# Two groups of value sums in a row, every eight steps, in a three-stage attention kernel

## The chip, the cores and the metric

The kernel runs on one core of one Trainium2 chip. The metric is the device time of one execution in microseconds; times of instructions come from one profiled execution.

## What is computed

Tokens (16 sequences of 512, width 128) are embedded, mixed by a low-rank attention, and sent through a block with three attentions of 8 heads of 16: a "spatial" one (S) and a causal "temporal" one (T), whose weights a router picks per sequence, and a cross attention (C) between their outputs. A feed-forward layer follows.

```python
att = jax.nn.softmax(jnp.einsum('bthd,bshd->bhts', q, k), axis=-1)
o = jnp.einsum('bhts,bshd->bthd', att, v).reshape(B, T, D)
...
spatial_out = _spatial_experts(xn, idx_s, ...)
temporal_out = _temporal_experts(xt, idx_t, ...)
fused = _cross_mha(spatial_out, temporal_out, ...)
x = x + fused
```

## The kernel before

Three programs run one after the other: `embed_and_mix`, `attend` and `feed_forward`. The change lies in `attend`, which takes most of the time. Its work is 48 units: S, T and C for each of 16 sequences, and a unit has 32 tiles (8 heads by 4 blocks of 128 tokens).

Each engine runs a list written out by hand. Time is counted in slots of 32 steps; three slots make a batch (`units` says which sequences meet in a slot). In a slot TensorE (PE) scores one unit (`score`, line 1265, bf16, one tile per step), makes the logits of the unit scored in the slot before (`logits`, line 1285, tile n - 8 at step n, so the last eight tiles fall into the first eight steps of the next slot), and weighs the values with its probabilities (`weigh`, line 1304). I call a slot by the unit that is scored in it: in the T slot T is scored, and the logits and sums are first C's and then S's; in the C slot they are S's, then T's; in the S slot T's, then C's. At a step the order on PE is: transpose of the maxima (1274), projections of the next unit (1248 and 1252, steps 3, 9 and 12 to 15), logits, group of sums, score, output projection (1321 and 1324, steps 29 and 30).

- **Scores** go to a ring of `RL` = 3 PSUM banks. VectorE (DVE) reduces each to its row maxima (`reduce`, lines 1066 and 1070); the score of tile n waits until tile n - 3 has been reduced.
- **Logits** go to a second ring of `RC` = 3 banks. ScalarE (ACT) turns them into probabilities in SBUF (`exponential`, line 1170); the logits of tile n wait for the exponential of tile n - 3. Causal T tiles are narrower (512, 384, 256 or 128 columns).
- **Groups.** Four tiles of probabilities make a group, 8 groups a unit. `weigh` runs four fp32 matmuls with 32 columns of weights each, side by side in the array, into one PSUM bank (`sums`). A T group also waits for GpSimd (POOL) to zero the future on its diagonal block (`zero_future`, line 939). The probabilities have `RP` = 3 buffers of one group each, so the first exponential of a group waits for the sums of the group three before it.
- **Evictions.** After groups 3 and 7 ACT empties the bank: a Ln (`s_all`, `s_high`) and, one exponential later, a copy (`u_all`, `u_high`). Groups 0 and 4 wait for these. DVE then shuffles the sums (`swap`, step 21), ACT takes the reciprocal (`reciprocal`, step 24), and POOL multiplies.

Two rules of waiting that the steps below rest on:

```python
at_least(pe, reduced, TILES * u + n - RL + 1)      # in score
at_least(pe, exped, TILES * u + n - RC + 1)        # in logits
pe.wait_ge(exped, TILES * u + 4 * q + 4)           # in weigh, S and C
pe.wait_ge(cut, 2 * NB * b + q + 1)                # in weigh, T
at_least(act, summed, 8 * u + n // 4 - RP + 1)     # in exponential, n % 4 == 0
```

In the order before, group q is weighed at step 17 + 4q: groups 0 to 3 at steps 17, 21, 25 and 29 of a slot, groups 4 to 7 at steps 1, 5, 9 and 13 of the next. The evictions stand at ACT's steps 30 and 31 (groups 0 to 3) and 14 and 15 (groups 4 to 7).

Of the kernel before, what the change touches and what calls it, by code (L numbers as in the profile page):

```python
# [38 lines left out]
TURN_AT, KEEP_MAXIMA_AT = (19, 6), (18, 5)  # L39
PROJECT_AT = (3, 9, 12)  # L40
KEPT_AT = (4, 10)
WEIGH_AFTER = 9
VALUES_AT = 16
GROUP_1_AT, GROUP_2_AT = (30, 31), (14, 15)
SWAP_AT, RECIP_AT = 21, 24
OUTPUT_AT, KEEP_AT = 29, 31
PROJECT_PARTS, OUTPUT_PARTS = (1, 1, 4), 2
LAG = 8
# [20 lines left out]
def exists(b):  # L69
    return not isinstance(b, int) or 0 <= b < B  # L70
# [14 lines left out]
def desk_use(name, b):  # L85

    if name[0] in "qkv" and name[1] == "S" and isinstance(b, int) and b == 0:
        return "qkv".index(name[0])
    i = b - DESK_BATCH[name]
    order = [u for s in DESK for u in s]  # L90
    at = order.index(name)
    if isinstance(i, int):
        return desk_count(i) + sum(exists(i + DESK_BATCH[u]) for u in order[:at])
    return DESK_FIRST + DESK_USES * (i - STEADY[0]) + at


def unit_no(kind, b):

    if kind == "C":
        return 3 * B - 1 if isinstance(b, int) and b == B - 1 else 3 * b + 4  # L100
    if isinstance(b, int) and b == 0:
        return "ST".index(kind)
    return 3 * b - 1 + "ST".index(kind)
# [10 lines left out]
def group_place(kind, b, q):  # L114

    return ring_place(kind, b, 4 * q, 4 * RP) // 4


def at_least(eng, sem, value):

    if not isinstance(value, int) or value > 0:
        eng.wait_ge(sem, value)
# [568 lines left out]
def attend(nc, shared, s_in, s_out, t_in, t_out, c_in, c_out, c_bias):  # L691
# [3 lines left out]
    with ExitStack() as ctx:  # L695
# [90 lines left out]
        def units(i, slot):  # L786

            return ((("T", i), ("S", i), ("C", i - 2), ("T", i - 1)),
                    (("C", i - 1), ("T", i), ("S", i), ("C", i - 2)),
                    (("S", i + 1), ("C", i - 1), ("T", i), ("S", i)))[slot]  # L790
# [19 lines left out]
        def first_key(kind, tile):  # L810

            return P * (tile // 4 % NB) if kind == "T" else 0
# [41 lines left out]
        with nc.Block() as block:  # L854
# [370 lines left out]
            def _(pe):  # L1225
# [31 lines left out]
                def score(kind, b, n):  # L1257

                    u = unit_no(kind, b)
                    if n == 0:  # L1260
                        pe.wait_ge(stack_in[kind], 16 * 2 * NPROD * (b + 1))
                    at_least(pe, reduced, TILES * u + n - RL + 1)
                    hd, tb = n // NB, n % NB
                    keys = P * (tb + 1) if kind == "T" else T
                    nc.tensor.matmul(psum[:, ring_place(kind, b, n, RL), 0:keys], qs[kind][0:RA, hd, P * tb:P * tb + P],  # L1265
                                     ks[kind][0:RA, hd, 0:keys], start=True, stop=True).then_inc(scored, 1)

                def turn_maxima(kind, b, half):

                    if not exists(b):  # L1270
                        return
                    pe.wait_ge(reduced, TILES * unit_no(kind, b) + HALF * (half + 1))
                    at_least(pe, desk_free, desk_use("hm"[half] + kind, b))
                    nc.tensor.transpose(desk[0:HALF, 0:P], mx[kind][:, HALF * half:HALF * half + HALF], ident[:])\
                        .then_inc(desk_full, 1)

                def logits(kind, b, n):

                    u = unit_no(kind, b)
                    if n % HALF == 0:  # L1280
                        pe.wait_ge(rows_in[n // HALF][kind], 16 * NPART * (b + 1))
                    at_least(pe, exped, TILES * u + n - RC + 1)
                    hd, s, t0 = n // 16 * 4 + n % 4, n // 4 % NB, first_key(kind, n)
                    bank = LOGITS + ring_place(kind, b, n, RC)
                    nc.tensor.matmul(psum[:, bank, t0:T], ks[kind][0:RB, hd, P * s:P * s + P],  # L1285
                                     qs[kind][0:RB, hd, t0:T], start=True, stop=True).then_inc(logits_in, 1)

                def weigh(kind, b, q):

                    u = unit_no(kind, b)  # L1290
                    g, s = q // NB, q % NB
                    if kind == "T":
                        pe.wait_ge(cut, 2 * NB * b + q + 1)
                    else:
                        pe.wait_ge(exped, TILES * u + 4 * q + 4)
                    if q == 0:
                        pe.wait_ge(v_ready[kind], b + 1)
                        pe.wait_ge(desk_free, desk_use("v" + kind, b) + 1)
                        at_least(pe, high_out, u)
                    if q == NB:  # L1300
                        pe.wait_ge(low_out, u + 1)
                    t0 = first_key(kind, 4 * q)
                    for j in range(4):
                        last = nc.tensor.matmul(sums[32 * j:32 * j + 32, t0:T], va[kind][:, s, g, j, :],  # L1304
                                                probs[:, group_place(kind, b, q), j, t0:T], start=(s == 0),
                                                stop=(kind == "T" or s == NB - 1), skip_group_check=(kind == "T"))
                    last.then_inc(summed, 1)
# [21 lines left out]
                def slot_program(i, slot):  # L1329
                    (kn, bn), (ka, ba), (kb, bb), (ko, bo) = units(i, slot)  # L1330
                    for n in range(TILES):
                        if n == TURN_AT[0]:
                            turn_maxima(ka, ba, 0)
                        if n == TURN_AT[1]:
                            turn_maxima(kb, bb, 1)
                        for c in range(3):
                            if 0 <= n - PROJECT_AT[c] < PROJECT_PARTS[c]:
                                project(kn, bn, c, n - PROJECT_AT[c])
                        if n < LAG and exists(bo):
                            logits(ko, bo, TILES - LAG + n)  # L1340
                        if n >= LAG and exists(bb):
                            logits(kb, bb, n - LAG)
                        q, rest = divmod(n - LAG - WEIGH_AFTER, 4)
                        if rest == 0 and q < 0 and exists(bo):
                            weigh(ko, bo, q + 8)
                        if rest == 0 and q >= 0 and exists(bb):
                            weigh(kb, bb, q)
                        if exists(ba):
                            score(ka, ba, n)
                        if 0 <= n - OUTPUT_AT < OUTPUT_PARTS and exists(bo) and ko != "S":  # L1350
                            output(ko, bo, n - OUTPUT_AT)
# [14 lines left out]
                last.then_inc(folded, 1)  # L1366
                pe.wait_ge(fold_kept, 2)
                whole_loop(pe, slot_program)


# [247 lines left out]
```

## Time and profile before

| | before |
|---|---|
| median of 3 runs (lowest to highest) | 1627.6 us (1627.55 to 1627.78) |
| the profiled execution's own time | 1629.0 us |
| its span, first to last instruction | 1627.2 us |
| PE busy | 1510.4 us (93%) |
| DVE busy | 1241.3 us (76%) |
| ACT busy | 1129.1 us (69%) |
| POOL busy | 1000.1 us (61%) |
| mean granted clock of PE | 0.947 |

The busy times are those of the whole span, with the first and the last program in them. A matmul's row lasts until its last result is written, and the next one starts before that; the time that a matmul holds the array is therefore read from one start to the next, not from the length of the row. Start to start is what the text uses.

### The profile page before, as it was taken

What the parts mean: (1) busy time and instruction counts of PE and PEld (TensorE: products, weight loads), DVE (VectorE), ACT (ScalarE), POOL (GpSimd) and SP (SyncE); (2) the same over time, 40 slices, a digit from 0 to 9 for tenths busy, and PEclk for the clock granted to TensorE, in tenths of its full rate; (3) what the DMA queues carried; (4) which work ended last, traced back from release to release, by engine and by line L of the source; (5) the groups of instructions that cost most, each with busy time, mean ns of one, the idle gap of its engine ahead of it and who ended that gap; (6) DMA issues with size and microseconds to landing.
All of it is one profiled execution on the core that took longest, in us unless ns stands there. A gap on an engine that the chain in (4) does not pass through costs nothing. (4 is left out here: it accounts for less than half of the span.)

```text
span 1627.2 us, 37445 instructions
## 1 busy us (share of the span) xinstructions
PE 1510.4 (93%) x8694; PEld 661.2 (41%) x8694; DVE 1241.3 (76%) x3412; ACT 1129.1 (69%) x2201; POOL 1000.1 (61%) x1359
## 2 busy tenths in 40 slices
PE   4779948899999999999999999999999999975999
PEld 1239932233333333343333333333333343211777
DVE  6868858579888887979888887979788888452772
ACT  5756734567787878787787878787787878824433
POOL 7704443856777776866767776856767775432553
PEclk9879958889999999999999999999999999967999
DMA  3311153645654655655655655655655643030222
GB/s 83 105 31 46 46 81 50 87 71 74 80 81 61 88 69 65 86 69 72 80 77 64 88 65 69 85 68 74 80 75 66 88 59 64 2 40 28 59 71 65
DMA packets 140021, 110.34 MB, mean 68 GB/s; under 512 B 22721, under 2 KB 134465, under 8 KB 139969
## 3 DMA queue, kind: packets, MB, share of 16 engines
q1 hardware_dynamic: 137920, 105.53, 44.0%
q0 software_dynamic: 2048, 4.20, 1.0%
q8 instruction: 23, 0.38, 0.1%
q14 instruction: 30, 0.24, 0.1%
HBM read 19.29 MB, written 8.39 MB: 17 GB/s over the span
## 5 line engine op out<-in xcount | busy, mean ns | idle before, releaser
L1170 ACT ACTIVATE probs<-psum 128x512 f32<-128x512 f32 (+3 forms) x1536 | 755.2, 548 | 226.8 <-PE psum L1285 216.2
L1070 DVE TENSOR_REDUCE mx_S<-psum 128x1 f32<-128x512 f32 x512 | 326.2, 681 | 47.5 <-PE psum L1265 45.8
L1070 DVE TENSOR_REDUCE mx_C<-psum 128x1 f32<-128x512 f32 x512 | 317.8, 676 | 45.1 <-PE psum L1265 45.1
L1066 DVE CUSTOM_DVE_ANT_0 psum<-psum,causal 128x128 f32<-128x128 f32 (+3 forms) x512 | 242.8, 510 | 100.6 <-PE psum L1265 97.8
L1265 PE MATMUL psum<-ks_S,qs_S 96*128 96x512 bf16 x512 | 196.9, 395 | 10.3 <-DMA ks_S<-parts_k 6.0
L1265 PE MATMUL psum<-ks_C,qs_C 96*128 96x512 bf16 x512 | 199.6, 398 | 4.3 <-DMA ks_C<-parts_k 1.2
L1285 PE MATMUL psum<-qs_C,ks_C 99*128 99x512 bf16 x512 | 189.3, 385 | 3.6 <-ACT probs L1170 3.2
L1285 PE MATMUL psum<-qs_S,ks_S 99*128 99x512 bf16 x512 | 190.6, 384 | 0.2
L951 POOL CAST parts_q<-f_q 128x512 bf16<-128x512 f32 x48 | 29.3, 610 | 227.6 <-ACT f_q L1161 227.1
L1265 PE MATMUL psum<-ks_T,qs_T 96*128 96x128 bf16 (+3 forms) x512 | 156.7, 309 | 1.7 <-DVE mx_S L1070 0.9
L1285 PE MATMUL psum<-qs_T,ks_T 99*128 99x256 bf16 (+3 forms) x512 | 153.3, 305 | 2.1 <-ACT probs L1170 1.0
L1304 PE MATMUL psum<-probs,va_S 128*32 128x512 f32 x1024 | 136.4, 604 | 1.7 <-ACT u_all L1190 0.6
L1304 PE MATMUL psum<-probs,va_C 128*32 128x512 f32 x1024 | 136.9, 607 | 0.8 <-ACT u_all L1190 0.6
L1265 PEld LDWEIGHTS psum<-ks_C,qs_C 96*128 96x128 bf16 x512 | 49.8, 97 | 166.6 <-DVE mx_C L1070 124.2
L939 POOL TENSOR_SCALAR_AFFINE_SELECT probs<-probs 128x512 f32<-128x512 f32 x128 | 81.0, 633 | 56.6 <-ACT probs L1170 54.5
L1265 PEld LDWEIGHTS psum<-ks_S,qs_S 96*128 96x128 bf16 x512 | 50.1, 98 | 153.5 <-DVE mx_S L1070 104.4
L1265 PEld LDWEIGHTS psum<-ks_T,qs_T 96*128 96x128 bf16 x512 | 50.5, 99 | 137.0 <-DVE mx_T L1066 93.0
L1304 PE MATMUL psum<-probs,va_T 128*32 128x512 f32 (+3 forms) x1024 | 97.7, 454 | 2.4 <-POOL probs L939 1.4
L1517 ACT ACTIVATE gT<-psum,b 128x512 f32<-128x512 f32 x64 | 44.0, 687 | 80.4 <-PE psum L1537 80.4
L1005 POOL TENSOR_TENSOR s_all<-s_all,s_high 128x512 f32<-128x512 f32 x48 | 60.9, 1269 | 23.4 <-ACT u_high L1180 23.4
L316 POOL DMA_INDIRECT h<-in_table,ids x64 | 60.6, 947 | 20.3 <-issue 19.2
L1285 PEld LDWEIGHTS psum<-qs_C,ks_C 99*128 99x128 bf16 x512 | 49.4, 98 | 58.2 <-ACT probs L1170 23.9
(186 smaller groups left out, 2723.3 us busy)
## 6 DMA issues: line engine op xcount, KB each, us to landing
qs_S<-parts_q SPq DMA_DIRECT2D x96, 128.0 KB, 4.4
ks_S<-parts_k SPq DMA_DIRECT2D x96, 128.0 KB, 5.1
qs_T<-parts_q SPq DMA_DIRECT2D x96, 128.0 KB, 4.4
ks_T<-parts_k SPq DMA_DIRECT2D x96, 128.0 KB, 4.6
qs_C<-parts_q SPq DMA_DIRECT2D x96, 128.0 KB, 4.5
ks_C<-parts_k SPq DMA_DIRECT2D x96, 128.0 KB, 4.9
w_in_S<-in_s_in SPq DMA_DIRECT2D x16, 257.0 KB, 2.7
w_in_T<-in_t_in SPq DMA_DIRECT2D x16, 257.0 KB, 2.7
```

Source lines behind the costliest of these rows:

```text
L316: nc.gpsimd.indirect_dma_start(h[:, NB * b + n, :], None, table, bass.IndirectOffsetOnAxis(ap=ids[:, NB * b + n:NB * b + n + 1].bitcast(U3 ...
L939: nc.gpsimd.affine_select(out=diagonal, in_=diagonal, compare_op=ALU.is_ge, fill=0.0, base=0, pattern=[[0, 4], [1, P]], channel_multiplier ...
L951: nc.gpsimd.tensor_copy(parts[c][:, 0, :], f32[c][:]).then_inc(hi_done, 1)
L1005: nc.gpsimd.tensor_tensor(s_all[:], s_all[:], s_high[:], ALU.add).then_inc(s_merged, 1)
L1066: nc.vector.tensor_tensor_reduce(tile[:, 0:last_key], tile[:, 0:last_key], causal[:, T - last_key:T], 1.0, NEG, ALU.add, ALU.max, mx[kind] ...
L1070: nc.vector.tensor_reduce(mx[kind][:, n:n + 1], tile, AX_X, ALU.max, negate=True).then_inc(reduced, 1)
L1170: nc.scalar.activation(probs[:, group_place(kind, b, n // 4), n % 4, t0:T], psum[:, LOGITS + ring_place(kind, b, n, RC), t0:T], ACT.Exp, s ...
L1265: nc.tensor.matmul(psum[:, ring_place(kind, b, n, RL), 0:keys], qs[kind][0:RA, hd, P * tb:P * tb + P], ks[kind][0:RA, hd, 0:keys], start=T ...
L1285: nc.tensor.matmul(psum[:, bank, t0:T], ks[kind][0:RB, hd, P * s:P * s + P], qs[kind][0:RB, hd, t0:T], start=True, stop=True).then_inc(log ...
L1304: last = nc.tensor.matmul(sums[32 * j:32 * j + 32, t0:T], va[kind][:, s, g, j, :], probs[:, group_place(kind, b, q), j, t0:T], start=(s == 0),
L1517: nc.scalar.activation(gT[:, odd, f, :], psum[:, 1 + f, :], ACT.Gelu, bias=b1[:, f:f + 1])\
```

## The change

Groups are weighed in pairs: groups 0 and 1 at step 19, 2 and 3 at step 27, 4 and 5 at step 3 of the next slot, 6 and 7 at step 11. The evictions move two steps ahead, to ACT's steps 28 and 29, and 12 and 13. `RP`, `RL` and `RC` stay at 3.

```diff
-WEIGH_AFTER = 9
+PAIR_AT = 19
 VALUES_AT = 16
-GROUP_1_AT, GROUP_2_AT = (30, 31), (14, 15)
+GROUP_1_AT, GROUP_2_AT = (28, 29), (12, 13)
...
-                        q, rest = divmod(n - LAG - WEIGH_AFTER, 4)
-                        if rest == 0 and q < 0 and exists(bo):
-                            weigh(ko, bo, q + 8)
-                        if rest == 0 and q >= 0 and exists(bb):
-                            weigh(kb, bb, q)
+                        pair, rest = divmod(n - PAIR_AT, 8)
+                        for q in (2 * pair, 2 * pair + 1):
+                            if rest == 0 and q < 0 and exists(bo):
+                                weigh(ko, bo, q + 8)
+                            if rest == 0 and q >= 0 and exists(bb):
+                                weigh(kb, bb, q)
```

On PE, in the S slot of the steady loop, this stood around group 2 of C (`va_C` are C's values, the ISA rows are PE's own waiting and counting), at step 25:

```order
L1285 MATMUL psum<-qs_C,ks_C 128x512
L1295 ISA
L1304 MATMUL psum<-probs,va_C 32x512 x4
L122 ISA
L1265 MATMUL psum<-ks_S,qs_S 128x512
```

Now groups 2 and 3 stand in the same list at step 27, with eight scores and eight logits, instead of four and four, between them and the pair before:

```order
L1285 MATMUL psum<-qs_C,ks_C 128x512
L1295 ISA
L1304 MATMUL psum<-probs,va_C 32x512 x4
L1295 ISA
L1304 MATMUL psum<-probs,va_C 32x512 x4
L122 ISA
L1265 MATMUL psum<-ks_S,qs_S 128x512
```

Group 3 stood four steps behind group 2, with four scores and four logits between them; now it stands directly behind it.

On ACT, in the T slot of the steady loop, right behind the key projection's copy (`f_k`, step 10), the eviction of groups 4 to 7 stood after four exponentials:

```order
L1167 ISA
L1170 ACTIVATE probs<-psum 128x512
L1167 ISA
L1170 ACTIVATE probs<-psum 128x512
L1167 ISA
L122 ISA
L1170 ACTIVATE probs<-psum 128x512
L1167 ISA
L1170 ACTIVATE probs<-psum 128x512
L1176 ISA
L122 ISA
L1178 ACTIVATE s_high<-psum,high,low 128x512
```

Now, from `f_k` on, it stands after two:

```order
L1161 ACTIVATE f_k<-psum,w_in_C 128x512
L1167 ISA
L1170 ACTIVATE probs<-psum 128x512
L1167 ISA
L1170 ACTIVATE probs<-psum 128x512
L1176 ISA
L122 ISA
L1178 ACTIVATE s_high<-psum,high,low 128x512
L1167 ISA
L122 ISA
L1170 ACTIVATE probs<-psum 128x512
L1180 ACTIVATE u_high<-psum,high 128x512
```

The Ln and its copy have moved ahead of two exponentials; the copy is still one exponential behind the Ln.

## Rows read from the trace of the kernel before

**Rows 1.** Stretches of a batch: length, busy PE, PEld, DVE, ACT, POOL, clock, DMA
```profile
843.50:849.58 6.08, 6.08 (x37) 2.11 (x36) 3.37 (x14) 5.09 (x10) 4.04 (x6) 1.00 0.34 77
849.58:855.84 6.26, 6.17 (x43) 2.83 (x41) 4.75 (x20) 5.59 (x11) 5.68 (x9) 1.00 1.06 121
855.84:860.90 5.06, 5.06 (x34) 1.70 (x32) 4.47 (x21) 4.39 (x9) 4.16 (x7) 1.00 0.97 99
860.90:874.87 13.97, 13.96 (x79) 5.23 (x78) 10.30 (x26) 11.22 (x22) 7.17 (x10) 1.00 0.14 27
801.49:807.68 6.19, 6.19 (x42) 2.92 (x41) 5.49 (x11) 4.83 (x11) 5.81 (x8) 1.00 1.11 121
807.68:813.02 5.34, 5.20 (x34) 1.73 (x33) 5.34 (x13) 3.21 (x10) 5.01 (x9) 1.00 0.86 88
813.02:824.61 11.59, 11.45 (x71) 4.14 (x71) 10.43 (x18) 8.51 (x21) 8.34 (x11) 1.00 0.24 53
824.61:830.66 6.05, 6.05 (x43) 3.02 (x41) 5.86 (x11) 5.54 (x11) 5.39 (x10) 1.00 0.88 106
830.66:836.35 5.69, 5.69 (x33) 1.71 (x32) 5.40 (x13) 4.75 (x10) 5.28 (x8) 1.00 0.93 107
836.35:843.50 7.15, 7.15 (x39) 2.83 (x38) 6.22 (x14) 5.84 (x11) 1.32 (x2) 1.00 0.14 37
```

**Rows 2.** PE in the steady part (start:end, length, PE busy, clock, DMA)
```profile
375.64:1378.66 1003.02, 997.96 (x5991) 1.00 0.56 74
```

**Rows 3.** PE timeline around one group, S slot (start, length, line, operation)
```profile
831.10 0.38 PE L1265 MATMUL psum<-ks_S,qs_S 96*128 96x512 bf16 x1
831.31 0.38 PE L1285 MATMUL psum<-qs_C,ks_C 99*128 99x512 bf16 x1
831.62 1.06 PE L1304 MATMUL psum<-probs,va_C 128*32 128x512 f32 x8
832.62 0.39 PE L1265 MATMUL psum<-ks_S,qs_S 96*128 96x512 bf16 x1
```

**Rows 4.** PE timeline, the second pass of the same group alone
```profile
832.08 0.61 PE L1304 MATMUL psum<-probs,va_C 128*32 128x512 f32 x4
```

**Rows 5.** DVE timeline: shuffle, ten reductions without a gap, one that waited
```profile
810.49 0.71 DVE L1107 STREAM_SHUFFLE s_right<-s_all 128x512 f32<-128x512 f32 x1
...
811.11 6.04 DVE L1070 TENSOR_REDUCE mx_C<-psum 128x1 f32<-128x512 f32 x10
...
833.05 0.69 DVE L1070 TENSOR_REDUCE mx_S<-psum 128x1 f32<-128x512 f32 x1 [0.29 <-PE psum L1265]
```

**Rows 6.** PE timeline, a score that waited for a reduction, C slot
```profile
811.83 0.39 PE L1265 MATMUL psum<-ks_C,qs_C 96*128 96x512 bf16 x1
```

**Rows 7.** ACT timeline: reciprocal, exponentials, Ln and copy, T slot
```profile
859.41 0.63 ACT L1197 ACTIVATE s_recip<-s_right 128x512 f32<-128x512 f32 x1
859.95 3.02 ACT L1170 ACTIVATE probs<-psum 128x512 f32<-128x512 f32 x6
863.10 0.78 ACT L1187 ACTIVATE s_all<-psum,low,high 128x512 f32<-128x512 f32 x1
...
864.35 0.68 ACT L1190 ACTIVATE u_all<-psum,low 128x512 f32<-128x512 f32 x1
864.92 0.60 ACT L1170 ACTIVATE probs<-psum 128x512 f32<-128x512 f32 x1
```

**Rows 8.** PE timeline beside them: logits that waited, score behind the group
```profile
861.56 0.39 PE L1285 MATMUL psum<-qs_S,ks_S 99*128 99x512 bf16 x1
...
862.87 0.28 PE L1265 MATMUL psum<-ks_T,qs_T 96*128 96x256 bf16 x1
```

**Rows 9.** PE timeline, a projection and what follows it, S slot
```profile
818.12 1.02 PE L1248 MATMUL psum<-xt,w_in_T 128*128 128x512 f32 x2
818.98 0.27 PE L1285 MATMUL psum<-qs_T,ks_T 99*128 99x256 bf16 x1
```

**Rows 10.** POOL timeline, the mask of T's group 5
```profile
816.96 0.63 POOL L939 TENSOR_SCALAR_AFFINE_SELECT probs<-probs 128x512 f32<-128x512 f32 x1
```

## The prediction

> **What bounds the kernel now.** I read the table by stretches first. A batch of the steady part is cut at the scores of steps 3, 11, 19 and 27 of its three slots; "T 20–27" is the stretch from the score of step 19 to that of step 27 in the slot where T is scored (the slots C and S follow) [rows 1]. The reader is to see three things there: the clock is 1.00 in all ten rows; PE is busy 73.0 of 73.38 us (sum of the rows), so PE sets the pace; but DVE is busy 61.6 us (84%) and ACT 59.0 us (80%), and in C 20–27 DVE is busy the whole 5.34 us. PE leads by little. The steady part lasts 1003.02 us [rows 2], 1003.02 / 73.38 = 13.67 batches. Then PE's timeline around one group of sums shows what a group costs beside its streaming [rows 3, 4], and the timelines of DVE, of ACT and of PE where it waits for them show how fast each can follow [rows 5 to 8].
>
> **The switch that is removed.** A logits matmul holds PE for 0.21 to 0.22 us (831.10 to 831.31), yet the group after the one at 831.31 starts only at 831.62, 0.10 late, and the next score comes 1.00 later [rows 3]. Streaming is 0.86 of that: two fp32 passes over 512 columns, as in the projection from 818.12 to 818.98 [rows 9]. So each group costs 1.00 + 0.10 = 1.10 us, of which 0.10 + 0.14 = 0.24 is getting into and out of the 32-column form. No two groups stand in a row in this trace, so the second one's saving has to be bounded: nothing, if every group pays for itself; 0.24, if it streams straight on. The nearest row is the border between the two passes inside a group: the second begins 0.46 after the first, 0.03 more than its 0.43 of streaming [rows 4]. I take 0.24 - 0.03 = 0.21 per pair. The Trainium skill, TensorEngine Tiling (Array Packing), Key Properties, says that changing the tiling mode drains the engine and changing only the tile does not; by it the whole 0.24 would be saved, 0.03 more per pair, and the sum below would come to 1646.
>
> A batch has 24 groups, so 12 pairs: 12 x 0.21 = 2.52 us of PE, 34 us in 13.67 batches, if PE goes on setting every stretch. From the start of the last logits before it to the next score, a full pair takes 0.22 + 2 x 1.10 - 0.21 = 2.21 us, where a single group took 1.31 (831.31 to 832.62) [rows 3].
>
> **What moves without a price.** A tile's exponential that reuses a probability buffer needs the group three back; PE runs that group one step ahead of the tile's logits, so waiting for the logits covers it. The T groups need POOL's mask: group 5's ends at 816.96 + 0.63 = 817.59 [rows 10]. In the new order its pair starts after the projection and logits of step 3, which without the 1.00 us of the single group at step 1 is 818.98 + 0.11 - 1.00 = 818.1, and group 5 comes second, some 0.9 later: 1.4 us of cover. If POOL were later than that, PE would stand with scores and logits behind it. The evictions keep their four instructions and their place behind groups 3 and 7; where they land among the exponentials is priced next. No DMA changes its place, nor does anything in SP's and POOL's lists.
>
> **What the pair collides with.** Scores and logits have three PSUM banks each. The nth score waits for the reduction of score n-3, the nth logits for the exponential of tile n-3. DVE starts 0.43 after a score that it was waiting for (832.62 to 833.05) [rows 3, 5], takes 0.60 per tile (ten in 6.04) and 0.62 for the shuffle (810.49 to 811.11) [rows 5]; a waiting score starts 0.72 after the reduction that frees its bank began (811.11 to 811.83) [rows 5, 6]. ACT takes 0.48 per exponential (six in 3.02, the last running 0.6), 0.54 for the reciprocal, 1.25 for the Ln of an eviction with one exponential and 0.57 for its copy; the Ln starts 0.23 after the score behind its group, and logits follow 0.05 after the end of the exponential that frees their bank (859.95 + 2 x 0.48 + 0.60 = 861.51, logits at 861.56) [rows 7, 8]. ACT's start after logits I take as DVE's, 0.43.
>
> With a group every 4 steps, three banks bridge it: 1.31 us against 3 x 0.60. With a pair every 8 steps the followers starve for over 2 us, and then PE must push eight tiles through three banks before the next pair. The eighth score waits for the fifth reduction: 0.43 + 4 x 0.60 + 0.72 = 3.55 us after the pair, and PE can do nothing else, since the pair stands behind it in its queue.
>
> S 20–27: 3.55 + 0.62 (shuffle) + 0.22 + 2.21 = 6.60, before 5.69.
> T 20–27, by ACT: first logits 0.23, exponential at 0.66, four of them 1.92, reciprocal 0.54, fifth ends at 3.72, last logits at 3.77, + 2.21 = 5.98, before 5.06.
> T 12–19, by ACT: Ln at 0.23, + 1.25 + 0.57, three exponentials 1.44, the fifth 0.60, + 0.05 = 4.14, + 2.21 = 6.35, before 6.26.
> C 20–27, by DVE with a pair of 256 and 128 columns (0.64 instead of 1.71 of streaming): 3.55 + 0.62 + 0.22 + 1.14 = 5.53, before 5.34.
> C 12–19, by DVE: 3.55, score 0.22, transpose 0.11, pair of 512 and 384 columns behind 256-column logits 2.21 - 0.32 = 1.89: 5.77, before 6.19.
> C 28 to S 11, by DVE: 3.55 + 0.22 + projection 0.86 + 1.89 = 6.52; then its sixth score waits until 0.43 + 1.20 + 0.72 = 2.35, + 2.02 for a projection and five bf16 matmuls, + 1.14 = 5.51. Together 12.03, before 11.59.
> By PE: T 4–11 6.08 - 0.21 = 5.87; T 28 to C 11 13.97 - 0.42 = 13.55; S 28 to T 3 7.15 - 0.21 = 6.94; S 12–19 takes a full group for one of 128 columns, 6.05 + 0.64 - 0.21 = 6.48, before 6.05.
>
> Sum after: 5.87 + 6.35 + 5.98 + 13.55 + 5.77 + 5.53 + 12.03 + 6.48 + 6.60 + 6.94 = 75.10, +1.72 per batch; x 13.67 = +23.5 us. The start and the end of the middle stage I leave as they are. The profiled execution took 1629.0 us with a span of 1627.2; 1629.0 + 23.5 = 1652.5, and as the median of the runs lies 1.4 below that execution, 1651.
>
> Bounds: with the full 0.24 the pairs cost 12 x 0.03 x 13.67 = 5 us less, 1646; with no saving 12 x 0.21 x 13.67 = 34 us more, 1685. If the banks cost nothing, 1627.6 - 34 = 1593.
>
> **The rivals.** A (slower still): every group goes on paying its own switch; 1685. For it: no row shows two groups in a row. Against it: the second pass inside a group pays 0.03 only. In that case the change doesn't remove what it is there to remove.
> B (faster): PE's saving reaches the end, 1593. For it: PE busy 73.0 of 73.38. Against it: DVE at 84% with C 20–27 full already. It decides by the price of the banks: my sum has 1.72 + 2.52 = 4.2 us per batch for them, and below 2.5 the change gains. It would be smaller if DVE or ACT entered the stretches less empty than I have them. The rule of the Trainium skill named above is this rival's reason as far as PE goes; the border inside a group is all that the trace has to bear it out.
> C (no change): the banks cost just the 2.5 us; 1628.
>
> **How the numbers follow.** Forecast 0.68, A 0.08, B with its smaller forms 0.18, C 0.06. About 0.2% (3.3 us) is what a measurement here can tell from no change. Slower 0.68 + 0.08 = 0.76, same 0.06, faster 0.18. The range leaves out the far half of B and the upper half of A: 1612 to 1684. The forecast's own range is 1635 to 1667: some 0.3 of the 4.2 us, 1.2, either way (1.2 x 13.67 = 16).
>
> **What would show it.** Right: the steady batch grows from 73.38 to about 75.1; two groups in a row from the first one's start to the next score in about 1.9 us; S 20–27 and T 20–27 near 6.6 and 6.0, with PE's scores there waiting for reductions, logits for exponentials; DVE and ACT idle after each pair. Wrong: a pair near 2.2 us (A); stretches 20–27 under 5.7 and 5.1 (B); T groups waiting for POOL's mask.

## The result and the profile after

| | before | after |
|---|---|---|
| median of 4 runs (lowest to highest) | 1627.6 us (1626.67 to 1627.78) | 1731.1 us (1728.1 to 1734.42) |
| span of the profiled execution | 1627.2 us | 1726.7 us |
| PE busy | 1510.4 us (93%) | 1524.5 us (88%) |
| DVE busy | 1241.3 us (76%) | 1232.1 us (71%) |
| ACT busy | 1129.1 us (69%) | 1106.5 us (64%) |
| mean granted clock of PE | 0.947 | 0.952 |

The change makes the kernel slower by 6.3%: after over before is 1.0633 (95% interval 1.0617 to 1.0649). The sign is the forecast one, the size is four times as much: +103.6 us where +23.5 was forecast, and 1731 lies outside the range of 1612 to 1684. All three engines have a smaller share of the span, so most of the lost time is waiting.

The stretches of a batch show where. These are windows of the kernel after, cut as in [rows 1], from the score of step 3, 11, 19 or 27 to the next of them: first the T slot (the last row runs on to step 11 of the C slot), then an earlier C and S slot.

```profile
887.63:893.72 6.09, 6.02 (x40) 2.25 (x37) 3.96 (x17) 4.70 (x9) 5.36 (x10) 1.00 0.47 84
893.72:900.75 7.03, 6.52 (x45) 3.00 (x42) 4.78 (x19) 5.44 (x10) 6.04 (x8) 1.00 1.12 119
900.75:906.95 6.20, 5.42 (x36) 1.84 (x33) 4.43 (x19) 4.59 (x9) 4.08 (x6) 1.00 0.51 51
906.95:921.08 14.13, 13.88 (x81) 5.37 (x78) 10.17 (x23) 10.64 (x20) 6.84 (x11) 1.00 0.22 35
...
841.02:848.05 7.03, 6.01 (x46) 3.21 (x42) 5.76 (x11) 4.16 (x10) 6.68 (x9) 1.00 1.10 122
848.05:853.58 5.53, 4.58 (x36) 1.78 (x33) 5.11 (x11) 3.47 (x9) 3.20 (x6) 1.00 0.44 45
853.58:860.25 6.67, 6.34 (x38) 2.17 (x35) 5.28 (x9) 4.78 (x12) 4.27 (x6) 1.00 0.15 39
860.25:865.74 5.49, 5.28 (x39) 2.20 (x35) 5.06 (x9) 3.15 (x9) 4.50 (x8) 1.00 0.42 76
865.74:873.25 7.51, 6.81 (x45) 3.20 (x41) 5.97 (x12) 5.84 (x12) 7.02 (x10) 1.00 1.00 121
873.25:879.87 6.62, 5.97 (x36) 1.89 (x33) 5.53 (x11) 4.64 (x9) 4.18 (x6) 1.00 0.53 81
879.87:887.63 7.76, 7.27 (x42) 2.94 (x39) 4.99 (x12) 5.93 (x11) 0.32 (x1) 1.00 0.03 9
```

The clock is 1.00 in every row, and a batch lasts 80.1 us where 73.4 stood. Set beside the forecast, stretch by stretch:

| stretch | before | forecast | after | after less forecast |
|---|---|---|---|---|
| T 4–11 | 6.08 | 5.87 | 6.09 | +0.22 |
| T 12–19 | 6.26 | 6.35 | 7.03 | +0.68 |
| T 20–27 | 5.06 | 5.98 | 6.20 | +0.22 |
| T 28 to C 11 | 13.97 | 13.55 | 14.13 | +0.58 |
| C 12–19 | 6.19 | 5.77 | 7.03 | +1.26 |
| C 20–27 | 5.34 | 5.53 | 5.53 | 0 |
| C 28 to S 11 | 11.59 | 12.03 | 12.16 | +0.13 |
| S 12–19 | 6.05 | 6.48 | 7.51 | +1.03 |
| S 20–27 | 5.69 | 6.60 | 6.62 | +0.02 |
| S 28 to T 3 | 7.15 | 6.94 | 7.76 | +0.82 |
| batch | 73.38 | 75.10 | 80.06 | +4.96 |

Where a stretch was forecast from the rings of three banks behind a pair (T, C and S 20–27), the forecast is right to 0.02 us twice and to 0.22 once. T 20–27, the one with 0.22, it had held by ACT alone; there PE waits for DVE's reductions too (`mx_T`, twice, 0.6 us in that window). What is missing sits in the stretches 12–19, which end with step 19, and in those around step 3. 4.96 us by 13.67 batches are 68 of the 80 us by which the forecast fell short. Another 7 lie behind the steady part, 1.3 in one C slot in which the clock fell (last section), and 4 between the profiled executions and the medians.

The view of waits names the work there. This is the kernel after, PE, from 500 to 1300 us, ten batches: us in total, times, longest.

```profile
PE psum L1274 <- DVE va_S L1091: 8.7, 10, 0.9
PE psum L1265 <- DVE mx_C L1070: 8.4, 22, 0.6
PE psum L1265 <- DVE mx_S L1070: 7.4, 16, 0.7
PE psum L1265 <- DVE mx_T L1066: 6.3, 20, 0.4
PE psum L1274 <- DVE va_T L1091: 6.2, 10, 0.6
PE psum L1248 <- DVE t_outT L1130: 4.9, 10, 0.5
PE psum L1274 <- DVE va_C L1091: 3.7, 9, 0.4
PE psum L1248 <- DVE X L1137: 2.5, 10, 0.3
```

For the kernel before the same view of the same window has no row at all. The three rows of L1265 are scores that wait for a reduction, which the forecast has in the slots C and S. The five others it does not have: the transpose of the maxima (L1274) and the first projection (L1248) wait until DVE has copied out what stood in a bank before them. That is one single PSUM bank, `desk` in the code, through which every small product of a slot goes in turn: projections, transposed maxima, values, output projection. Each is written by PE, read by DVE or ACT, and only then may PE write the next.

At step 19 of the S slot one sees it happen. PE of the kernel after (start, length, line, operation, in brackets the idle time and what ended it):

```profile
869.10 0.39 PE L1285 MATMUL psum<-qs_C,ks_C 99*128 99x512 bf16 x1
869.32 0.38 PE L1265 MATMUL psum<-ks_S,qs_S 96*128 96x512 bf16 x1
869.58 0.39 PE L1285 MATMUL psum<-qs_C,ks_C 99*128 99x512 bf16 x1
869.81 0.38 PE L1265 MATMUL psum<-ks_S,qs_S 96*128 96x512 bf16 x1
870.81 0.28 PE L1274 MATMUL psum<-ident,mx_S 128*16 128x128 f32 x1 [0.62 <-DVE va_T L1091]
870.93 0.39 PE L1285 MATMUL psum<-qs_C,ks_C 99*128 99x512 bf16 x1
871.40 1.92 PE L1304 MATMUL psum<-probs,va_C 128*32 128x512 f32 x16
873.25 0.39 PE L1265 MATMUL psum<-ks_S,qs_S 96*128 96x512 bf16 x1
```

and DVE beside it:

```profile
870.01 0.74 DVE L1091 TENSOR_TENSOR va_T<-psum,w_in_T 128x256 f32<-128x256 f32 x2
870.68 1.28 DVE L1070 TENSOR_REDUCE mx_S<-psum 128x1 f32<-128x512 f32 x2
...
873.68 0.69 DVE L1070 TENSOR_REDUCE mx_S<-psum 128x1 f32<-128x512 f32 x1 [1.54 <-PE psum L1265]
```

The same place before, on PE:

```profile
828.67 1.06 PE L1304 MATMUL psum<-probs,va_C 128*32 128x512 f32 x8
...
830.11 0.38 PE L1265 MATMUL psum<-ks_S,qs_S 96*128 96x512 bf16 x1
830.33 0.27 PE L1274 MATMUL psum<-ident,mx_S 128*16 128x128 f32 x1
```

and on DVE:

```profile
829.33 0.74 DVE L1091 TENSOR_TENSOR va_T<-psum,w_in_T 128x256 f32<-128x256 f32 x2
```

DVE copies the values at its step 16, a reduction or two behind PE. Before, the group at step 17 held PE from 828.67 to 829.66, the copy was over at 830.07, and the transpose of step 19 found the bank free at 830.33. After, nothing long stands between steps 16 and 19: PE comes to the transpose at 869.81 + 0.22 = 870.03, when the copy has just begun, and stands until 870.81. That is 0.78 late (the view says 0.62, since the modelled end of the score before reaches into the wait). All logits, the pair and all scores stand behind it in PE's queue, and the pair of 1.85 us that could have covered the copy comes only after it. DVE, which was the late one, is then idle for 1.54.

At step 3 it is the first projection. PE and then DVE of the kernel after, T slot:

```profile
883.68 0.33 PE L1265 MATMUL psum<-ks_T,qs_T 96*128 96x384 bf16 x1
884.51 1.12 PE L1248 MATMUL psum<-oT_S,w_fold 128*128 128x512 f32 x2 [0.49 <-DVE t_outT L1130]
```

```profile
883.52 0.74 DVE L1130 SCALAR_TENSOR_TENSOR t_outT<-psum,w_out_T,xres 128x512 f32<-128x512 f32 x1
```

DVE reads the output projection of step 30 at its step 31. Before, the group at step 1 covered that. Now the next group is the pair at step 3, and the projection of step 3 stands ahead of it.

The pair itself does what it was to do: from 871.40 to the next score at 873.25 are 1.85 us, where two groups apart took 2 x 1.00 + 0.10 [rows 3]. It saves the whole 0.24, not the 0.21 that I took. The rule that the prediction cites from the Trainium skill, TensorEngine Tiling (Array Packing), Key Properties, gives the whole 0.24; the trace agrees with it.

### The profile page after: what moved, and what is told of

It is laid out like the page before. It is cut to its first block and busy times, and to the rows that moved or that the text cites. A ratio compares the mean times of both kernels' runs of the same rounds, so it can differ in the third digit from the quotient of the medians.

```text
span 1726.7 us, 37444 instructions
## 1 busy us (share of the span) xinstructions
PE 1524.5 (88%) x8693; PEld 684.7 (40%) x8694; DVE 1232.1 (71%) x3412; ACT 1106.5 (64%) x2201; POOL 1003.7 (58%) x1359
## 5 line engine op out<-in xcount | busy, mean ns | idle before, releaser
L1170 ACT ACTIVATE probs<-psum 128x512 f32<-128x512 f32 (+3 forms) x1536 | 734.3, 559 | 316.3 <-PE psum L1285 312.8
L1070 DVE TENSOR_REDUCE mx_S<-psum 128x1 f32<-128x512 f32 x512 | 321.4, 681 | 84.3 <-PE psum L1265 82.4
L1265 PE MATMUL psum<-ks_S,qs_S 96*128 96x512 bf16 x512 | 198.3, 397 | 23.0 <-DVE mx_S L1070 13.8
L1265 PE MATMUL psum<-ks_C,qs_C 96*128 96x512 bf16 x512 | 199.1, 399 | 17.6 <-DVE mx_C L1070 13.0
L1265 PE MATMUL psum<-ks_T,qs_T 96*128 96x128 bf16 (+3 forms) x512 | 155.6, 306 | 14.5 <-DVE mx_T L1066 9.9
L1304 PE MATMUL psum<-probs,va_C 128*32 128x512 f32 x1024 | 125.7, 609 | 1.2
L1304 PE MATMUL psum<-probs,va_S 128*32 128x512 f32 x1024 | 123.1, 598 | 0.8
L1265 PEld LDWEIGHTS psum<-ks_C,qs_C 96*128 96x128 bf16 x512 | 49.9, 98 | 144.0 <-DVE mx_C L1070 84.3
L1265 PEld LDWEIGHTS psum<-ks_S,qs_S 96*128 96x128 bf16 x512 | 50.0, 98 | 138.0 <-DVE mx_S L1070 81.4
L1265 PEld LDWEIGHTS psum<-ks_T,qs_T 96*128 96x128 bf16 x512 | 49.9, 98 | 113.7 <-issue 56.8
L1304 PE MATMUL psum<-probs,va_T 128*32 128x512 f32 (+3 forms) x1024 | 83.1, 442 | 1.9 <-issue 0.5
L1285 PEld LDWEIGHTS psum<-qs_S,ks_S 99*128 99x128 bf16 x512 | 50.0, 98 | 64.3 <-ACT probs L1170 38.0
```

Of the source, the lines that this page charges most:

```text
L1070: nc.vector.tensor_reduce(mx[kind][:, n:n + 1], tile, AX_X, ALU.max, negate=True).then_inc(reduced, 1)
L1170: nc.scalar.activation(probs[:, group_place(kind, b, n // 4), n % 4, t0:T], psum[:, LOGITS + ring_place(kind, b, n, RC), t0:T], ACT.Exp, s ...
```

## The experiments

In the expectations H is the theory that PE loses the time at hand-overs of that one bank which a single group used to cover. Its rivals are named there: that the rings of three banks cost more than forecast (R), that the moved evictions cost it (E), that a pair costs something by itself (G). A ratio is to the kernel before.

### The transpose behind the pair

```diff
-TURN_AT, KEEP_MAXIMA_AT = (19, 6), (18, 5)
+TURN_AT, KEEP_MAXIMA_AT = (20, 6), (19, 5)
```

> The changed kernel with the transposes of the first 16 maxima one step later (step 20, their copy behind reduction 19), so that they stand behind the pair of step 19 instead of ahead of it. Theory H (hand-over): PE stands at step 19 because the desk bank still holds the values that VectorE copies out at its step 16, and the pair stands behind that wait; before, a single group at step 17 covered it. H expects the three waits of 0.9, 0.6 and 0.4 us per batch and the restarts behind them to go: 2 to 3 us per batch, 27 to 41 us in all, 1687 to 1701. Rival R (banks): the loss is all the starving of the three PSUM banks, and another wait takes the place of this one: 1722 to 1735.

1708.0 us, ratio 1.0489 (1.0468 to 1.0510): 23 us less than the change. The three rows of `va_*` are gone from the view of waits, and the stretches 12–19 came down to 6.41 (T), 5.79 (C) and 6.62 us (S), against 6.35, 5.77 and 6.48 in the prediction, which still has the transpose (0.11) in them. With the wait gone the forecast is right there to some 0.2. The stretches 20–27, into which the transpose has moved, grew by 0.15 to 0.18. A batch fell from 80.1 to 77.8 us, 31 us in all, which is what H expected. But the time lies above H's range, for in the C slot of every other batch PE's clock fell, and such a batch lasts 79.1; six of them take back 8 us. One window shows it:

```profile
837.84:844.62 6.78, 5.76 (x38) 2.06 (x34) 5.89 (x13) 3.71 (x9) 5.01 (x9) 0.81 0.59 61
```

### The projection behind the pair

```diff
-PROJECT_AT = (3, 9, 12)
+PROJECT_AT = (4, 9, 12)
```

> The changed kernel with the first projection one step later (step 4), behind the pair of step 3. H: the projection waits for VectorE's last use of the desk bank at its step 31; before, the single group at step 1 covered it. H expects the waits of 0.5 and 0.3 us per batch and their restarts to go: 0.8 to 1.5 us per batch, 11 to 20 us, 1708 to 1718. R: 1722 to 1735.

1719.2 us, ratio 1.0558 (1.0537 to 1.0579): 12 us less than the change, as much as H expected at the least, though the time lies 1 us above its range. `t_outT` and `X` are gone from the waits. A new row has come in: the second transpose, at step 6, now follows the projection by two steps and waits for ACT's copy of it (L1274 <- ACT f_q, 6.0 us, 20 times).

### Both

```diff
-TURN_AT, KEEP_MAXIMA_AT = (19, 6), (18, 5)
-PROJECT_AT = (3, 9, 12)
+TURN_AT, KEEP_MAXIMA_AT = (20, 6), (19, 5)
+PROJECT_AT = (4, 9, 12)
```

> The changed kernel with both the transposes at step 20 and the first projection at step 4. H as the runs so far have it: the two gains of 23 and 12 us add up, 1690 to 1702, less what a new uncovered hand-over costs: between the projection at 4 and the transposes at 6 only two steps are left, so they will wait for ScalarE's copy of the query projection, which could give back up to 0.6 us per slot, 25 us. R: one of the two gains is lost to the banks, 1705 to 1720.

1693.9 us, ratio 1.0403 (1.0381 to 1.0426), 37 us less than the change, where the two alone had given 23 and 12: they add up. A batch lasts 76.9 us, where the clock doesn't fall; of the 4.96 that it had over the forecast 1.84 are left.

### Pairs one step sooner

```diff
-PAIR_AT = 19
+PAIR_AT = 18
-GROUP_1_AT, GROUP_2_AT = (28, 29), (12, 13)
+GROUP_1_AT, GROUP_2_AT = (27, 28), (11, 12)
```

> The changed kernel with the pairs one step sooner (18, 26, 2, 10) and the evictions one step sooner (27 and 28, 11 and 12): the pair stands between the value projection and the transposes, and between the output projection and the next first projection, as the single groups did. H: both hand-overs are covered again and what stays is the price of the banks as the prediction had it, a batch of about 75.1 us: 1648 to 1665. R: the same length of pair against the same three banks, 1720 to 1735. A T group that waits for GpSimd's mask, whose cover gets a step shorter, could add up to 1 us per batch, 14 us, to either.

A miss: 1708.2 us, ratio 1.0483 (1.0466 to 1.0501). The rows of `va_*`, `t_outT` and `X` are gone, as meant, but others have come in (waits of PE from 500 to 1300):

```profile
PE psum L1274 <- ACT f_q L1161: 8.9, 30, 0.4
...
PE psum L1304 <- POOL probs L939: 5.1, 10, 0.5
```

With the pair at step 2, no group stands between the projection of step 3 and the transpose of step 6. The same bank waits, at another of its hand-overs, and a T pair now comes before POOL's mask. Moving the pairs moves the uncovered hand-over; it doesn't remove it. PE's clock also fell in most batches of this run (78.6 to 78.8 us, against 77.6 in the two without), so that the waits are not all of the miss.

### The bank's uses spread out

```diff
-TURN_AT, KEEP_MAXIMA_AT = (19, 6), (18, 5)
-PROJECT_AT = (3, 9, 12)
-KEPT_AT = (4, 10)
+TURN_AT, KEEP_MAXIMA_AT = (20, 7), (19, 6)
+PROJECT_AT = (4, 10, 12)
+KEPT_AT = (5, 11)
```

> The changed kernel with the uses of the desk bank set around the pairs: first projection at 4, second transposes at 7, key projection at 10, first transposes at 20, each behind a pair or three steps from the use before. H: most hand-over waits go, what stays is the price of the banks and 0.3 us here and there: a batch of 75.1 to 77, 1650 to 1680. R: 1700 or more.

A miss too: 1710.2 us, ratio 1.0494 (1.0475 to 1.0512), in the range that the expectation gives to R, and 16 us worse than the transpose and the projection alone. ACT's copy of the projection moved a step later along with the transpose that waits for it, so that wait grew (L1274 <- ACT f_q, 11.9 us, 30 times) instead of going, and T groups wait for POOL's mask (4.8 us, 10 times). These two rows are 10.6 us more in ten batches, and a batch lasts 78.0 us instead of 76.9; the rows of the rings are those of the run with both users moved, so the number is R's but the cause is not.

### The evictions where they were

```diff
-GROUP_1_AT, GROUP_2_AT = (28, 29), (12, 13)
+GROUP_1_AT, GROUP_2_AT = (30, 31), (14, 15)
```

> The changed kernel with the evictions back at steps 30 and 31, 14 and 15. H: nothing to do with the loss, 1718 to 1740. Rival E (evictions): their Ln now stands ahead of the first exponential after a pair and holds up the logits' banks; with them back the time falls by over 25 us, below 1705.

1743.3 us, ratio 1.0706 (1.0650 to 1.0761): slower still, so E falls. It rests on two executions, 1735.6 and 1751.0, the lower one just above the slowest of the change (1734.4). Logits now wait more for exponentials:

```profile
PE psum L1285 <- ACT probs L1170: 28.4, 68, 0.6
```

Of the hand-over rows only `va_S` is left (3.8 us), yet the batch is no shorter, 80.4 us against 80.1: one wait has taken the place of the other. The earlier evictions don't cost the change its time; by the batch they save it 0.3 us.

### Reductions over half the columns

```diff
-nc.vector.tensor_reduce(mx[kind][:, n:n + 1], tile, AX_X, ...)
+nc.vector.tensor_reduce(mx[kind][:, n:n + 1], tile[:, 0:T // 2], AX_X, ...)
...
-                                         scale=SCALE).then_inc(exped, 1)
+                                         scale=SCALE / 64).then_inc(exped, 1)
```

> The changed kernel with VectorE's S and C reductions over 256 of the 512 columns (and the exponential's scale divided by 64 against overflow): the maxima are those of half the keys, so the output is not the reference's. A reduction then takes about half of its 0.60 us. Both H (hand-over of the desk bank) and R (three banks) hold VectorE for the slow follower in the slots C and S; both expect S 20-27 and C 20-27 to fall to what PE sets, near 5.5 and 4.7 us, and the slot T to stay at 26.9: a batch of 74.5 to 77.5, 1650 to 1695. If VectorE were not the cause, 1720 or more. H alone expects the wait of the transposes in the slot T (0.6 us per batch) to stay.

1662.2 us, ratio 1.0209 (1.0187 to 1.0231), inside the expected range. S 20–27 fell to 6.05 and C 20–27 to 4.56, and the T slot, whose reductions are untouched, kept its stretches. But the hand-over rows fell with them (`va_S` from 8.7 to 5.7), since it is DVE that is late at both. The run shows that DVE's time behind a pair sets the pace; it does not tell H from R. In the T slot the row of the transposes (`va_C`) did stay, 4.1 us against 3.7, as H alone had expected, but it is the smallest of the three. (The 0.6 of the expectation is `va_T`, which belongs to the S slot and fell to 2.3 us.)

### The kernel before, with the hand-overs uncovered

```diff
-TURN_AT, KEEP_MAXIMA_AT = (19, 6), (18, 5)
-PROJECT_AT = (3, 9, 12)
+TURN_AT, KEEP_MAXIMA_AT = (17, 6), (18, 5)
+PROJECT_AT = (1, 9, 12)
```

Here the groups stand alone as before, every four steps. Only the transpose and the projection go to the steps of the groups that covered them, where they stand ahead of the group.

> The kernel BEFORE, with its single groups every four steps, but with the transposes at step 17 and the first projection at step 1, so that they stand ahead of the group of their step and no group covers the hand-over of the desk bank. The banks see the same bursts as before. H: PE waits for VectorE's value copy at step 17 and for its last copy at step 1, 0.4 to 1.0 us in each of six places a batch, 2.4 to 6 us per batch, 33 to 82 us: 1660 to 1710. R: nothing is lost, 1625 to 1635.

1819.1 us, ratio 1.1169 (1.1149 to 1.1189). No pair is left, and the kernel is slower than the change. H's direction, at more than twice the size. Two of the rows of waits, 500 to 1300:

```profile
PE psum L1274 <- DVE va_C L1091: 16.0, 10, 1.7
...
PE psum L1248 <- DVE t_outT L1130: 13.5, 10, 1.4
```

The waits are longer here, up to 1.7 us, than the 0.3 to 0.9 of the change, since the two users also stand two steps closer to the copies that they wait for. And PE's clock fell 25 times between 400 and 1400 us (last section); at the 1.25 us that a fall costs in the run with both users moved, an estimate, that is some 30 of the 191 us. H's numbers had neither.

### One pair in a gap of the kernel before

```diff
+                        if ko == "T" and n in (9, 13):
+                            rest = 1
+                        if ko == "T" and n == 11 and exists(bo):
+                            weigh(ko, bo, 6)
+                            weigh(ko, bo, 7)
```

> The kernel before, with one thing changed: T's groups 6 and 7 (256 and 128 columns) run in a row at step 11 of the S slot instead of 6 at step 9 or 10 and 7 later; every other group stands alone where it stood. Theory H (a pair saves its second group's switch, 0.24 us, and costs only where a hand-over of the desk bank or the ring of score banks loses its cover; here none does): once a batch, 13 to 14 times, so about 3 us less: 1623 to 1629. Rival G (whatever is paired in a row costs by itself, some 0.5 us a pair as the change's 75 us over 12 pairs a batch would have it): 1633 to 1638.

1628.4 us, ratio 1.0002 (0.9994 to 1.0011): G falls, and though the time is inside H's range, the 3 us that H had less are not there. The pair saves its 0.24, from 826.49 to 827.27, but the next group, at step 17, gives it back. PE:

```profile
826.49 0.86 PE L1304 MATMUL psum<-probs,va_T 128*32 128x256 f32 x16
827.27 0.39 PE L1265 MATMUL psum<-ks_S,qs_S 96*128 96x512 bf16 x1
...
831.18 1.07 PE L1304 MATMUL psum<-probs,va_C 128*32 128x512 f32 x8 [0.18 <-ACT u_high L1180]
```

The pair's 0.78 us stand where 0.57 + 0.36 + 0.09 = 1.02 stood. But group 7 has left its place between the logits of step 13 and group 0 of step 17. The eviction on ACT still stands behind the exponential of step 13, so PE comes to group 0 before ACT has copied the bank of sums out, and waits.

### The same with an earlier eviction

```diff
-                        if n in GROUP_2_AT and exists(bo):
-                            second_group(ko, bo, GROUP_2_AT.index(n))
+                        evict_at = (12, 13) if ko == "T" else GROUP_2_AT
+                        if n in evict_at and exists(bo):
+                            second_group(ko, bo, evict_at.index(n))
```

> The run with T's groups 6 and 7 in a row at step 11 of the S slot, and the eviction of T's groups 4 to 7 two exponentials sooner (steps 12 and 13 of the S slot). In the run before this one the pair took 0.24 us less than its two groups apart (826.49 to 827.27 against 0.57 + 0.36 + 0.09), and the group at step 17 waited 0.26 for the copy that empties the bank of sums. Theory H (the saving is real and was spent on that one wait): the wait goes, 0.24 x 13.7 = 3.3 us less than before: 1624 to 1627, ratio 0.997 to 0.999. Rival G (a pair saves nothing that reaches the end, whatever is ready behind it): ratio 1.000 within 0.001.

1628.9 us, ratio 0.9995 (0.9986 to 1.0004): inconclusive, its interval touches both. The wait for the copy is gone; ACT ends it at 825.61 + 0.73 = 826.34. Yet group 0 still starts late:

```profile
827.11 0.38 PE L1266 MATMUL psum<-ks_S,qs_S 96*128 96x512 bf16 x1
827.37 0.39 PE L1286 MATMUL psum<-qs_C,ks_C 99*128 99x512 bf16 x1
827.83 1.06 PE L1305 MATMUL psum<-probs,va_C 128*32 128x512 f32 x8
```

(This kernel has one line more: L1266 is the score, L1286 the logits, L1305 the group.)

It follows the logits by 0.46 where 0.31 is the rule [rows 3], and those logits come 0.26 behind their score instead of 0.22. The view of waits has no row for either. The 0.04 are ACT's: the logits start 0.06 after the end of the exponential that frees their bank (the second of two from 826.18 to 827.31), to which ACT comes straight from the eviction (last section). What holds the group for another 0.15 is not shown.

### Pairs between single groups

```diff
-TURN_AT, KEEP_MAXIMA_AT = (19, 6), (18, 5)
-PROJECT_AT = (3, 9, 12)
-KEPT_AT = (4, 10)
+TURN_AT, KEEP_MAXIMA_AT = (19, 7), (18, 6)
+PROJECT_AT = (3, 10, 12)
+KEPT_AT = (4, 11)
+EARLY_GROUPS_AT = {17: (0,), 23: (1, 2), 29: (3,)}
+LATE_GROUPS_AT = {1: (4,), 6: (5, 6), 11: (7,)}
...
-GROUP_1_AT, GROUP_2_AT = (30, 31), (14, 15)
+GROUP_1_AT, GROUP_2_AT = (30, 31), (12, 13)
...
```

(Against the kernel before. PE's list takes the groups of a step from the two tables.)

> The kernel before, with groups in a mixed order: one at step 17, two at 23, one at 29, one at 1, two short ones at 6, one at 11; the transposes of the maxima at 19 and 7, the projections at 3, 10 and 12, copies of the maxima at 18 and 6. Every use of the desk bank that waits for a copy has a group ahead of it, and no more than two groups stand together. Theory H (hand-overs without cover are what cost, pairs themselves save 0.24 us): two pairs a slot, six a batch, 1.44 us of 73.4, up to 20 us less: 1608 to 1625. If the two long groups at 23 still wait for the ring of score banks, as the forecast has it for the pairs, the saving is eaten by 0.3 to 0.6 us a slot: 1620 to 1640. Rival G (pairs cost by themselves, 0.5 us each): 1660 or more.

1644.5 us, ratio 1.0109 (1.0094 to 1.0123): just above H's second case, far below G's 1660. Six pairs a batch in place of twelve cost 16 us against the 1628.9 of the kernel before in that set of runs, not 104. No hand-over to the transposes or the first projection waits any more. What remains are scores that wait for reductions (`mx_T` 4.4 us, `mx_C` 4.2, from 500 to 1300), and 0.8 us at another hand-over of the same bank, the value projection behind ACT's `f_k`. T 20–27 lost 0.56 against the kernel before. But the two stretches C 4–19 together lasted 12.62 us instead of 12.85: there the whole 0.24 came through.

### Two pairs, everything covered

The kernel before, with the one pair and its early eviction, and in the C slot alone the places of the run above for groups 5 to 7:

```diff
+                        if ko == "S" and n in (6, 11) and exists(bo):
+                            for late in (5, 6) if n == 6 else (7,):
+                                weigh(ko, bo, late)
```

(`ko == "S"` is the C slot. The single groups of its steps 5, 9 and 13 go; the second transpose moves to 7, the key projection to 10 and its copy to 11, the eviction to 12 and 13.)

> The same, and in the C slot S's groups 5 and 6 in a row at step 6 and 7 at step 11, the transpose of S's second maxima at step 7, the projection of keys at 10, the eviction at 12 and 13; the groups at steps 17 to 29 alone. In the run with pairs between single groups the stretches C 3 to 19 lasted 12.62 where they had lasted 12.86, and lost nothing but in the stretches 19 to 27, which stay as before here. Theory H: two pairs a batch, 0.48 us of 73.4: 6.6 us less than before, 1620 to 1625, ratio 0.995 to 0.997. Rival G: ratio 1.000 within 0.001; rival R (a pair of two long groups, 1.86 us, always finds the rings of three banks empty behind it and loses 0.3 or more): ratio 1.001 to 1.004.

1624.2 us, against 1628.8 for the kernel before in the same set of runs: ratio 0.9971 (0.9961 to 0.9982). It is faster than both kernels, by somewhat less than H expected: a batch lasts 73.14 us instead of 73.39, half of the 0.48. Windows of C 4–11 and C 12–19:

```profile
864.50:872.02 7.52, 7.52 (x45) 2.44 (x44) 5.25 (x9) 5.59 (x11) 4.89 (x8) 1.00 0.26 49
872.02:877.12 5.10, 5.10 (x37) 2.85 (x34) 4.68 (x9) 4.09 (x10) 4.85 (x7) 1.00 1.10 121
```

PE is busy 12.62 of 12.62 us in the two C windows, with a pair of two full groups in them. So a pair in itself costs nothing: G falls, and so does the R of this run, a pair of two long groups that always loses behind itself. The saving reaches the end where what stands around the pair leaves nobody waiting. In the two stretches S 4–19 only 0.06 of the 0.24 came through (11.51 us instead of 11.57), little more than in the run with that pair alone, and there too logits follow the ends of exponentials.

## Why the prediction was wrong

**The direction and the rings were right.** PE's saving of twelve pairs is real, 0.24 instead of 0.21 each. Three banks don't bridge a pair: C 20–27 and S 20–27 came out at 5.53 and 6.62 for 5.53 and 6.60, with scores waiting for reductions. In T 20–27 the forecast had ACT for the slow one, and DVE was late as well. One term of C 28 to S 11 is 0.06 too large (0.86 + 5 x 0.22 is 1.96, not 2.02), 1 us in all. Rival A, that every group pays its own switch, falls with the 1.85 us of the pair; B and C fall with the time.

**The step that failed is "What moves without a price".** It went through the buffers of the probabilities, the mask and the evictions, and took it that whatever keeps its place in the lists keeps its price. It left out the bank `desk`: its hand-overs from PE to DVE or ACT and back keep their steps, but the change takes away the groups of steps 17 and 1 that stood between two of its uses. Those groups were not only work; they were the time in which DVE emptied the bank. That a transpose waits for `va_S` or a projection for `t_outT` could not be read as a wait from the trace of before, which has none. It could have been read as a margin: copy over at 829.33 + 0.74 = 830.07, transpose at 830.33, 0.26 us of slack, and the change takes a group of 1.00 us, with its switch 1.10, out from ahead of it. By that alone the transpose would have been 0.84 late; it was 0.78. (Group 7, 0.36 + 0.09 us at step 13, has left the same stretch, but DVE came to its copy as much sooner, 4.27 instead of 4.72 us behind the score of step 11.)

**What the runs put in its place.** The batch lost 4.96 us that the forecast does not have, most of it in the stretches 12–19 and around step 3. The five hand-over rows add up to 26.0 us in ten batches, 2.6 a batch; with the 0.16 that the view leaves out of each, five a batch, some 3.4. The rest goes with what follows such a wait: in S 12–19 the 1.03 over the forecast are 0.78 of waiting, 0.16 because the pair comes 0.47 after its logits and not 0.31, and two steps of 0.05 in which PE follows ACT (last section); the forecast had priced this stretch by PE alone. Moving the two users behind the pair gave back 23 and 12 us, together 37, and 3.1 of the 4.96 in the batch. Taking the cover away without any pair, with the users two steps closer to their copies besides, cost 191, of which some 30 are the clock.

**What stays open.** Of the 80 us that the forecast lacked, 37 came back so. With both users moved, 43 are still there. 1.84 us a batch, or 25 us, lie in the stretches: 0.17 to 0.37 in each stretch 20–27, and 0.72 around step 3 of the T slot, where the transpose waits for `f_q`, once more at the same bank. Some 6 us are the clock: five of the 13 C slots whose lengths I compared last 26.4 instead of 25.2 us, and in those five it fell (0.94 from 739.35 to 765.76 us, 1.00 from 817.62 to 842.80). Some 9 lie behind the steady part (248.6 us from its end to the end of the span before, 257.1 so, 255.5 with the change as it is) and 1.4 ahead of it; the last 1.4 are the profiled execution of before, which lay that much above its median. "The start and the end of the middle stage I leave as they are" was right for the start of the change and 7 us wrong for the end. I did not test what each of these parts is worth alone.

**Range and chances.** The range came from the bounds of the priced terms. A wait that is not in the list has no bound, and the only slower rival was about the switch.

## What to carry to other kernels

When work is moved out from between two uses of a shared buffer, go through every buffer that is handed back and forth across that place, also those whose own instructions don't move, and read the margin of each from the trace of before: when the copy ended, when the next writer came, how much work stood between. Gathering long instructions into fewer, longer bursts saves their switch only if each burst still lies over the copies that it used to hide; here two pairs a batch so placed gained 0.3%, and twelve on a regular grid lost 6.3%.

## What the hardware showed that I had not expected

**PE's clock fell behind long waits, and in some runs without any.** In the kernel before with its hand-overs uncovered, PE stood for 1.8 us ahead of a transpose, ran it and a group, and then went on at half the pace:

```profile
917.33 0.38 PE L1265 MATMUL psum<-ks_S,qs_S 96*128 96x512 bf16 x1
919.32 0.28 PE L1274 MATMUL psum<-ident,mx_S 128*16 128x128 f32 x1 [1.61 <-DVE va_T L1091]
...
921.97 0.63 PE L1265 MATMUL psum<-ks_S,qs_S 96*128 96x512 bf16 x1
922.40 0.63 PE L1285 MATMUL psum<-qs_C,ks_C 99*128 99x512 bf16 x1
```

A score and its logits are 0.43 apart there, where 0.22 is the rule. The windows of that stretch and the next:

```profile
921.00:924.40 3.40, 3.40 (x12) 1.04 (x9) 2.35 (x5) 1.56 (x3) 1.10 (x3) 0.55 1.12 114
924.40:929.00 4.60, 4.60 (x29) 1.32 (x28) 3.76 (x9) 3.51 (x8) 3.69 (x6) 1.00 0.02 3
```

The granted clock is 0.55, about the lower of the two levels (1.2 GHz), for some 3.4 us, and 1.00 (2.4 GHz) behind it. After the waits of under a microsecond in the kernel after, the windows of the batch shown stay at 1.00; in one C slot of that run, from 1230.13 to 1257.89 us, it was 0.94, and the slot lasts 27.8 instead of 26.5 us. With the transpose behind the pair it fell to 0.81 in the window shown, and so in every other batch, though no wait of PE's in that run was over 0.6 us in the view; what made it fall there is open.

**Steps at ACT's pace, which the view of waits doesn't show.** Between 868.84 and 869.81 the kernel after ran two steps of a score and a logits matmul in 0.48 and 0.49 us with no row in the view of waits, where 0.43 to 0.44 is the rule (831.10 to 831.31 is half a step [rows 3]). ACT's exponentials beside them, each line two in a row (the second of the first line is the first of the second):

```profile
867.91 1.13 ACT L1170 ACTIVATE probs<-psum 128x512 f32<-128x512 f32 x2
868.39 1.14 ACT L1170 ACTIVATE probs<-psum 128x512 f32<-128x512 f32 x2
```

The second ends at 867.91 + 1.13 = 869.04, the third at 868.39 + 1.14 = 869.53. They are tiles 6 and 7 of C, and the logits of tiles 9 and 10, which take over their banks, start at 869.10 and 869.58, 0.06 and 0.05 later; 0.05 is what the prediction read for logits that waited [rows 7, 8]. So PE follows ACT here at 0.48 us per exponential. ACT comes to these tiles straight from the eviction's Ln and copy (866.20 and 867.34), which the change put two exponentials earlier; that this place is what makes it late I did not test. Only the starts and ends side by side show such a wait; the view has no row for it.
